# Row maxima over 1024 keys from two double banks, three rotating banks instead of four, and four smaller edits to an attention and expert kernel

## The reference

```python
x = x + attention(layernorm(x))          # q, k, v: 256x256; rope on the last 256 tokens; softmax(q k / 4) v; output projection
h = layernorm(x)
scores = softmax(h @ gate_w.T)           # 16 experts; each takes its 128 best tokens of each sequence
x = x + sum over experts of (gelu(t @ Wg.T) * (t @ Wu.T)) @ Wd.T * score     # t: the tokens taken
      + (gelu(h @ Ws_g.T) * (h @ Ws_u.T)) @ Ws_d.T                           # shared expert, all tokens
```

## Time and profile before

| | before |
|---|---|
| time, three runs | 2406.83 us median (2402.03 to 2407.79) |
| profiled execution | 2401.16 us, its span 2399.3 us |
| busy over the span | PE 2218.2 us (92%), DVE 1883.3 us (78%), ACT 1561.1 us (65%), POOL 895.3 us (37%) |
| granted TensorE clock, mean | 0.976 |
| attention up to its last step | to about 1475 us |
| shared expert, matmuls | 1514 us to about 1795 us |
| experts | to the end |

### The profile page before, as it was taken

One profiled execution on the slowest core, in us unless ns is written; L12 is line 12 of the kernel. 1 busy time (PEld: TensorE's weight loads), 2 busy tenths in 40 slices (PEclk: granted clock), 3 DMA queues, 4 the chain that ended last, 5 costly groups with the idle time before them and its releaser, 6 DMA issues. The chain is left out here.

```text
span 2399.3 us, 42479 instructions
## 1 busy us (share of the span) xinstructions
PE 2218.2 (92%) x15630; PEld 1288.6 (54%) x15630; DVE 1883.3 (78%) x3505; ACT 1561.1 (65%) x3040; POOL 895.3 (37%) x1287
## 2 busy tenths in 40 slices
PE   4899999999999999999999987899997999999996
PEld 3233333333333333333343323788886888888886
DVE  4999999999999999999999994566663554555553
ACT  2499888898888898898898886333332343434332
POOL 4051362451451451542542230000004666666664
PEclk8799999999999999999999999899998999999998
DMA  4002013012022121111112111323223455454543
GB/s 112 5 25 34 17 41 69 17 48 62 16 62 50 29 63 34 34 58 34 34 43 32 34 43 38 132 87 97 79 71 104 90 112 115 87 111 109 108 94 36
DMA packets 206756, 147.81 MB, mean 62 GB/s; under 512 B 109952, under 2 KB 193792, under 8 KB 206592
## 3 DMA queue, kind: packets, MB, share of 16 engines
q1 hardware_dynamic: 182016, 112.08, 17.3%
q0 software_dynamic: 24576, 33.57, 8.1%
HBM read 78.50 MB, written 41.94 MB: 50 GB/s over the span
## 5 line engine op out<-in xcount | busy, mean ns | idle before, releaser
L515 DVE TENSOR_REDUCE sb_MX<-ring 128x1 f32<-128x512 f32 x2048 | 1281.9, 680 | 67.7 <-PE ring L800 51.5
L646 ACT ACTIVATE sb_PR<-rot 128x512 f32<-128x512 f32 x2048 | 1119.5, 608 | 145.7 <-PE rot L811 130.2
L800 PE MATMUL ring<-sb_KT,sb_QT 32*128 32x512 bf16 x2048 | 526.6, 391 | 92.3 <-DVE sb_MX L515 76.9
L822 PE MATMUL pv<-sb_PR,sb_VA 128*32 128x512 f32 x4096 | 546.5, 606 | 2.6 <-ACT sb_OT L696 0.6
L800 PEld LDWEIGHTS ring<-sb_KT,sb_QT 32*128 32x128 bf16 x2048 | 129.9, 91 | 707.4 <-DVE sb_MX L515 649.0
L811 PE MATMUL rot<-sb_QT,sb_KT 32*128 32x512 bf16 x2048 | 405.1, 386 | 0.9
L1113 ACT ACTIVATE ex_GL<-ex_gu 128x512 f32<-128x512 f32 x128 | 76.5, 597 | 348.6 <-PE ex_gu L63 346.4
L1180 DVE TENSOR_TENSOR ex_HF<-ex_GL,ex_gu 128x512 f32<-128x512 f32 x128 | 87.4, 682 | 252.0 <-ACT ex_GL L1113 252.0
L1077 POOL DMA_INDIRECT out<-ex_YS,ex_rows_out x128 | 208.9, 1632 | 44.1 <-issue 43.7
L1034 POOL TENSOR_TENSOR ex_pool_scratch<-identity 128x1 f32<-128x1 f32 x96 | 35.1, 366 | 472.4 <-POOLq L877 325.8
L61 PE MATMUL ex_gu<-ex_XH,weights_high 128*128 128x512 f32 x512 | 201.1, 393 | 2.4 <-DVE ex_XL L1172 2.4
(11 more groups left out here) (158 smaller groups left out, 4042.8 us busy)
## 6 DMA issues: line engine op xcount, KB each, us to landing
sb_XA<-x SPq DMA_DIRECT2D x8, 1024.0 KB, 5.7
sb_XR<-x SPq DMA_DIRECT2D x8, 1024.0 KB, 5.7
out<-sb_XR SPq DMA_DIRECT2D x8, 1024.0 KB, 4.6
xn<-sb_XN SPq DMA_DIRECT2D x8, 1024.0 KB, 4.4
sh_XG<-xn SPq DMA_DIRECT2D x16, 512.0 KB, 5.9
sh_X<-out SPq DMA_DIRECT2D x16, 512.0 KB, 5.2
weights<-WgT SPq DMA_DIRECT2D x16, 512.0 KB, 4.0
weights<-WuT SPq DMA_DIRECT2D x16, 512.0 KB, 6.4
```

The source lines that it names most:

```text
L515: nc.vector.reduce_max(MX[:, unit % 2, half, j, qt % 4:qt % 4 + 1], ring[m % RING][:], AX.X).then_inc(ring_done, 1)
L646: out = nc.scalar.activation(PR[V % P_STEPS][:, j, :], R[:], ACT.Exp, scale=0.25)
L800: nc.tensor.matmul(ring[m % RING][:], QT[g][r, P * qt:P * qt + P], KT[g][r, 512 * half:512 * half + 512], start=True, stop=True, tile_posi ...
L822: out = nc.tensor.matmul(pv_bank[head(j), :], VA[b % 2][:, kt, 4 * g + j, :], PR[V % P_STEPS][:, j, :], start=(kt == 0), stop=(kt == TT - 1))
```

## The change

- **Maxima.** The three ring banks become two tensors of two banks each (`ring`, [P, 1024]). A maximum is one reduction over 1024 keys from two matmuls of the same head; there are 1024 of them, two for a step, instead of 2048 and four. `join_halves` goes. `split_maxima` waits for the reductions themselves, and VectorE waits for `parts_ready` where it starts a unit.
- **Rotating banks.** `ROT` goes from 4 to 3.
- **TensorE's order in a step.** Row-wise and turned matmuls alternate: keys 0 to 511 of a check, turned head 0, keys 512 to 1023 of the same check and the same head, turned head 1; then `weigh_values`; then the same with the second check and turned heads 2 and 3.
- **Roots.** In the loop GpSimd computes the inverse roots (a power and one correction, six small operations at S = 7 and S = 27). Before the loop and in the tail VectorE keeps its Newton steps.
- **Turned tokens.** The turned second norm `XT` is also stored to device memory (`xn2T`, 1 MB for each sequence), and the shared expert loads its chunks from there. Its TensorE transposes go. ScalarE waits for that store at the first aot item of each later sequence.
- **Logits.** Four items of two 128-token tiles at S = 47 to 50 instead of two of four at S = 47 and 48. VectorE's and ScalarE's gate steps move two steps later.

```diff
-    ROT = 4
-    RING = 3
+    ROT = 3
+    RING = 2
-    CHECKS = 32 * UNITS * B
+    CHECKS = 16 * UNITS * B
...
-              43: (1, "k", 4), 44: (1, "q", 5), 45: (1, "k", 5), 47: (-1, "lg", 0), 48: (-1, "lg", 1),
+              43: (1, "k", 4), 44: (1, "q", 5), 45: (1, "k", 5), 47: (-1, "lg", 0), 48: (-1, "lg", 1), 49: (-1, "lg", 2),
+              50: (-1, "lg", 3),
...
     def check(m):
 
-        unit, n = m // 32, m % 32
-        return unit, (2, 3, 0, 1)[n % 4], n // 4 % 2, 4 * (unit % 2) + n // 8
+        unit, n = m // 16, m % 16
+        return unit, (2, 0, 3, 1)[n % 4], 4 * (unit % 2) + n // 4
...
-        ring = [ctx.enter_context(nc.psum_tensor(f"ring{i}", [P, 512], F32)) for i in range(RING)]
+        ring = [ctx.enter_context(nc.psum_tensor(f"ring{i}", [P, T], F32)) for i in range(RING)]
...
+            def store_turned(b):
+                sp.wait_ge(rot_done, done(("x2t", b, KH - 1, 1)))
+                sp.dma_start(d["xn2T"][bass.ds(b * H, H), :].rearrange("(k p) t -> p k t", p=P), XT[:]).then_inc(xt2_out, 16)
...
                 turn_maxima(n + 7)
                 if b < B - 1:
                     turn_maxima(n + 8)
+                if b:
+                    store_turned(b - 1)
...
+            def inverse_root(n, count):
+
+                y = rstd[n]
+                pool.wait_ge(mv_ready[n], count)
+                own.inc(nc.gpsimd.tensor_scalar(spread[:], mv[n][:, :, 1], EPS, None, ALU.add))
+                own.wait(pool)
+                own.inc(nc.gpsimd.tensor_tensor(y[:], spread[:], minus_half[:], ALU.pow))
+                own.wait(pool)
...
+                unit, j, qt = check(m)
+                if m % 16 == 0 and unit >= 2:
+                    dve.wait_ge(parts_ready, unit - 1)
+                dve.wait_ge(ring_full, 2 * m + 2)
+                nc.vector.reduce_max(MX[:, unit % 2, j, qt % 4:qt % 4 + 1], ring[m % RING][:], AX.X
                                      ).then_inc(ring_done, 1)
-
-            def join_halves(unit):
...
-                if more and 7 <= S <= 12:
-                    newton(0, 2 * (S - 7))
-                if prev and 26 <= S <= 31:
-                    newton(1, 2 * (S - 26))
...
+                    if kind == "aot" and b and h == 0 and half == 0:
+                        act.wait_ge(xt2_out, 16 * b)
...
-                m = 4 * (V + LEAD)
-                if m < CHECKS:
-                    score_rows(m)
-                    score_rows(m + 1)
-                if V >= 0:
-                    for j in range(2):
-                        score_turned(V, j)
+                m = 2 * (V + LEAD)
+                for n in range(2):
+                    if m < CHECKS:
+                        score_rows(m, n)
+                    if V >= 0:
+                        score_turned(V, n)
                 if V >= LAG:
                     weigh_values(V - LAG)
-                if m < CHECKS:
-                    score_rows(m + 2)
-                    score_rows(m + 3)
-                if V >= 0:
-                    for j in range(2, 4):
-                        score_turned(V, j)
+                for n in range(2):
+                    if m < CHECKS:
+                        score_rows(m + 1, n)
+                    if V >= 0:
+                        score_turned(V, 2 + n)
...
-                    sp.dma_start(XG[k % 2][:], rows("xn2", n)).then_inc(x_in[k % 2], 16)
+                        sp.wait_ge(xl_ready, n - 1)
+                    sp.dma_start(XG[k % 2][:], d["xn2T"][bass.ds(r * D, D), N * k:N * k + N].rearrange("(k p) t -> p k t", p=P)
+                                 ).then_inc(x_in[k % 2], 16)
...
-                    if not (last and k == K - 1):
+                    if not shared and not (last and k == K - 1):
                         turn_tokens(r if k < K - 1 else r + 1, (k + 1) % K)
```

More of the change, by code:

```diff
@@ L121, in attention @@
             + [("proj", B - 1, i) for i in range(TT)] + [("x2t", B - 1, h, half) for half in range(2) for h in range(KH)]
-            + [("lg", B - 1, half) for half in range(2)])
+            + [("lg", B - 1, n) for n in range(4)])
     ORDER = HEAD + [item for V in range(-LEAD, LAST)
@@ L210, in attention @@
         rstd_ready = [sem(f"rstd_ready{n}") for n in range(2)]
+        mv_ready = [sem(f"mv_ready{n}") for n in range(2)]
         xn_ready = [sem(f"xn_ready{h}") for h in range(2)]
@@ L326, in _ @@
             own = Tally(pool_own)
+            own.inc(nc.gpsimd.memset(minus_half[:], -0.5))
             for n in range(2):
@@ L454, in _ @@
                     clear_maxima(b + 1)
+                if more and S == 7:
+                    inverse_root(0, b + 1)
+                if b and S == 27:
+                    inverse_root(1, b)
                 if more and 13 <= S <= 16:
@@ L476, in gather_stats, with merge_stats @@
                     own.inc(nc.vector.bn_stats(stats[:, i, :], src[:, i, :]))
-            def merge_stats(n, tiles):
+            def merge_stats(n, tiles, last=False):
                 own.wait(dve)
                 for i in tiles:
-                    own.inc(nc.vector.bn_aggr(mv[n][:, i, :], stats[:, i, :]))
+                    step = nc.vector.bn_aggr(mv[n][:, i, :], stats[:, i, :])
+                    if last and i == tiles[-1]:
+                        step.then_inc(mv_ready[n], 1)
+                    else:
+                        own.inc(step)
             def newton(n, k):
@@ L592, in _ @@
                 if more and S in (4, 5):
-                    merge_stats(0, range(4 * (S - 4), 4 * (S - 3)))
-                if more and 7 <= S <= 12:
-                    newton(0, 2 * (S - 7) + 1)
+                    merge_stats(0, range(4 * (S - 4), 4 * (S - 3)), S == 5)
                 if prev and 21 <= S <= 24:
@@ L686, in empty @@
                 elif kind == "lg":
-                    _, b, half = item
+                    _, b, n = item
                     if b:
                         act.wait_ge(shifted_ready, b)
-                    out = nc.scalar.copy(LG[:, 4 * half:4 * half + 4, :], R[:, 0:4 * E].rearrange("p (t e) -> p t e", e=E))
+                    out = nc.scalar.copy(LG[:, 2 * n:2 * n + 2, :], R[:, 0:2 * E].rearrange("p (t e) -> p t e", e=E))
                 out.then_inc(rot_done, 1)
@@ L777, in fill @@
                 elif kind == "lg":
-                    _, b, half = item
-                    pe.wait_ge(rot_done, done(("x2t", b, 1, half)))
-                    for m in range(4):
-                        i = 4 * half + m
+                    _, b, n = item
+                    pe.wait_ge(rot_done, done(("x2t", b, 1, n // 2)))
+                    for m in range(2):
+                        i = 2 * n + m
                         for h in range(KH):
@@ L789, in head, with score_rows @@
                 return slice(QUAD * j, QUAD * j + QUAD)
[L791 to L793 removed]
+            def score_rows(m, half):
+                unit, j, qt = check(m)
                 b, g = unit // UNITS, unit % UNITS // 2
[L795 removed]
+                if m % 32 == 0 and half == 0:
                     pe.wait_ge(qk_turned[g], 32 * (b + 1))
[L797 removed]
+                if m >= RING and half == 0:
                     pe.wait_ge(ring_done, m - RING + 1)
                 r = head(j)
[L800 removed]
+                nc.tensor.matmul(ring[m % RING][:, 512 * half:512 * half + 512], QT[g][r, P * qt:P * qt + P], KT[g][r, 512 * half:512 * half + 512],
                                  start=True, stop=True, tile_position=(r.start, 0)).then_inc(ring_full, 1)
@@ L882, in sem @@
             return ctx.enter_context(nc.semaphore(tag + name))
-        XG = [sb(f"XG{c}", [P, CT, D], F32) for c in range(2)]
+        XG = [sb(f"XG{c}", [P, KD, N] if shared else [P, CT, D], F32) for c in range(2)]
         XH = [sb(f"XH{c}", [P, KD, N], FR) for c in range(2)]
@@ L1107, in split_tokens @@
                 n = r * K + k
-                act.wait_ge(turned_full, n + 1)
-                nc.scalar.copy(XH[k % 2][:], turned[:, :, 0:N]).then_inc(xh_ready, 1)
+                if shared:
+                    act.wait_ge(x_in[k % 2], 16 * (r + 1))
+                    if not (isinstance(n, int) and n < 2):
+                        act.wait_ge(gu_full, KF * (n - 1))
+                    nc.scalar.copy(XH[k % 2][:], XG[k % 2][:]).then_inc(xh_ready, 1)
+                else:
+                    act.wait_ge(turned_full, n + 1)
+                    nc.scalar.copy(XH[k % 2][:], turned[:, :, 0:N]).then_inc(xh_ready, 1)
             def gelu(n, f):
@@ L1334, in down @@
                 out.then_inc(y_full, 1)
-            turn_tokens(0, 0)
+            if not shared:
+                turn_tokens(0, 0)
             if shared:
```

57 lines of the change are left out of this document (26 added, 31 removed).

## The result

The changed kernel takes 2497.59 us (median of four runs, 2495.69 to 2516.54). The kernel before, run beside it, takes 2405.57 us (2402.03 to 2407.79). The ratio is 1.0402, 95% interval 1.0349 to 1.0454: slower by 4%. The forecast was 2500.0. The profiled execution of after took 2495.69 us, its span is 2493.7 and its mean granted clock 0.971 (before: 0.976).

What follows compares the result with a forecast made beforehand. DVE, near 97% busy, looked like the bound; after the change the rot-bank loop and PE would set the steps. 2401.2 + 92.4 + 8 + 13 - 2 - 13 + 1 = 2500.6, forecast 2500 us, range 2430 to 2540.

Steps and rivals of the forecast that it cites:

- Three banks: Attention steps: the loop through three rot banks takes 2.45 us, or 2.94 through the fourth exponential, whatever DVE's relief.
- Two matmuls of one head: Attention steps on PE: the second matmul waits 0.21 us for its strip, twice a step; one projection goes to 2.97.
- Maxima: DVE in attention: a maximum goes from 0.62 to about 1.14 us, bounds 1.13 and 1.24, a step from 2.47 to 2.28.
- Sum for a middle sequence: Its 64 steps total 189.2 us, plus 2 for late waits: 191.2 against 175.8; six sequences +92.4.
- Sequence 0 and the last: First and last sequences of attention, with fewer items: +8 us in sequence 0 and +13 in the last.
- Roots: Power operation on GpSimd in the loop: taken as 0; +5 us a sequence if the power took 10 us.
- Turned store: New 1 MB store: 0, or 2 to 3 us a sequence if late; shared expert without transposes: -13 us.
- Tail: End of attention: the last store lies beside the logits and gates, +1 us.
- DVE sets the pace: Rival: DVE still bounds attention, so each sequence gives back about 16 us; 2268 us, chance 0.08.
- Banks late and the matmuls side by side: Rival: banks bind but matmuls of one head overlap; 187 us a sequence, 2482 us, chance 0.15.
- Matmuls queue and the banks don't bind: Rival: matmuls of one head queue, banks don't bind; 179 us a sequence with waits, 2408 us, chance 0.07.
- The store or GpSimd late: Rival: late waits cost 3 us more for each of 7 sequences; 2521 us, chance 0.10.

Runs made afterwards that it cites:

- the kernel with the shorter product: Changed kernel, but from the second unit on the products with the values cover only 256 of 512 queries: 2481.05 us, ratio 1.0312.
- the small edits alone: Changed kernel with banks, ring, order and 512-key maxima of before, leaving GpSimd roots, turned tokens and four logit items: 2368.85 us, ratio 0.9843.
- the added matmuls: Changed kernel with row-wise matmuls kept up in the last 12 steps, their results unread: 2500.36 us, ratio 1.0392.
- the kernel with half the maxima: Changed kernel, but VectorE's maximum reads only keys 0 to 511 of each check: 2502.51 us, ratio 1.0401.
- the other head: Changed kernel, but the second 512 keys of a row-wise check come from the neighbouring head: 2469.95 us, ratio 1.0267.
- the product last: Changed kernel with weigh_values moved behind the second half of a step's score matmuls, ahead of the items: 2597.76 us, ratio 1.0798.
- run 26: Not a run's number: the words belong to "a run 26 to 28 us below the profiled one", a distance in time.

## Why the prediction was right

- **The bound.** That the engine with 97% was not what mattered after the change holds: DVE at 85% waits for PE, and at half its work nothing moves.
- **Three banks.** The loop was put at 2.45 and measures 2.42, and 2.94 with one more exponential measures 2.91 (transposes). The handovers together were taken 0.03 too long. In the kernel with three banks alone, without DVE's relief, it is 2.94. Shown by that run, by the length of the product (0.43 less in each kind of step) and by the product's place.
- **Two matmuls of one head.** Put at 0.21 twice a step; it is 0.21 (0.53 against 0.32, behind the product), shown with banks and without. The projection step came out at 2.97 as forecast. The prediction did not weigh that the two costs cover each other: with maxima over 512 keys they cost 15.4 us a sequence together, and undoing the order alone gives back 0.6, undoing the bank alone 4.3.
- **Maxima.** A maximum is 1.22 us long. The bounds of 1.13 and 1.24 were for the distance between starts, and that is 1.15 where eight run in a row (in the kernel with the shorter product), as forecast. In after it decides no step, so its cost does not matter.
- **Sum for a middle sequence.** Steps alone 189.2 forecast, and by the table 14 x 2.42 + 2 x 2.58 + 22 x 2.97 + 5 x 3.40 + 9 x 2.91 + 3 x 3.06 + 3.40 + 7 x 3.54 + 3.23 = 188.2; with the single late wait of 0.7 us that is the measured 188.8 within rounding. I had added 2 for late waits and found 0.7: PE's wait for GpSimd's split at S = 24. So 13.0 a sequence, where I had 15.4, and 78.0 in six where I had 92.4. This is the term that was too large, by 1.0 in the steps and 1.3 in the waits. Longer steps give DVE more time, so most of its late waits are gone (S = 23 takes 3.14 before and with the small edits alone, and 2.91 in after). At S = 8 it is the moved roots that help: with the small edits alone the wait is gone too.
- **Sequence 0 and the last.** +8 became +10.5, and +13 became +16.2. In the last, 4.2 of that is clock, which the added matmuls took away again: 12.0 without it. How much it is differs between executions: in the kernel with half the maxima, which has the same matmuls in these steps, the last sequence took 184.2. What is above 8 in sequence 0 was not tried by itself.
- **Roots.** Taken at 0. The power costs 1.67 us on GpSimd, and what follows it is not late:

```profile
667.42 1.67 POOL L423 TENSOR_TENSOR sb_rstd<-sb_spread,sb_minus_half 128x8 f32<-128x8 f32 x1
```

- **Turned store.** Taken at 0, and it is: ScalarE waits for no transfer in attention. Shared expert -13, measured -12.4 (-13.4 alone). Experts -1.2, not forecast.
- **Tail.** +1 became +4.9. Most of it is the clock. The gate logits of the last sequence, in after:

```profile
1601.77 6.85 PE L807 MATMUL rot<-sb_gw,sb_XT 128*128 128x16 f32 x32
```

Before, the same 32 matmuls took 4.04 us. In the kernels with the other head and the product last they took 4.11 and 3.77, and the tail 43.8 and 42.5 us; with 6.85 it is 45.0 to 46.9. So 2.8 of the 4.9 are there, and some 2 stay open.

That the total is this close is luck. The sum, 2500.6, started from the profiled execution of before, and the one of after took 2495.7, 4.9 less. In this, errors cancel: -14.4 in the middle sequences and -1.2 in the experts against +2.5, +3.2 and +3.9 in sequence 0, the last and the tail, and +1.1 in the stretch to the first product and the shared expert. The median, 2497.59, lies 1.9 above that execution, and the base lay 4.4 below the median of before. The mechanism, and each kind of step to 0.05 us, is what the runs bear out.

**The rivals.** DVE sets the pace: out. (Its sum takes 15 us a sequence where its text says 16, which would give 2260 and not 2268.) Banks late and the matmuls side by side, 2482: this is the kernel with the other head, at 2470 and 185.5 us a sequence where the rival had 187 without late waits. In after the two do queue, so it is out as well. Matmuls queue and the banks don't bind, 2408: with four banks the order alone gives 186.9 a sequence at full clock and not 179. That kernel lacks the wide maxima, which 2.3 us in steps without an item would need; but its steps with two items took 3.36, and not the 3.2 I had put there. The store or GpSimd late: one wait of 0.7 us.

## What to carry to other kernels

Before taking work off the engine that is busiest, follow the loop through the buffers (who frees the bank that who needs for what) and price it without any wait: if it is as long as the present step, the relief is worth nothing, and a bank less can cost more than all of it. Two changes that each lengthen the same step cost about as much together as the longer one alone, so take back both, or little of the gain shows. Small matmuls that are issued in one group should each have rows of the array of their own. It does not help to put one on other rows between two on the same rows: here the turned matmul between the two starts at once with the first, and the second still starts 0.22 us later.

## What the runs showed of the hardware

**The first 160 us.** The same work got the full clock at different times after the start. The stretch from 100 to 160 us of the kernel with half the maxima, and then of after:

```profile
100.00:160.00 60.00, 60.00 (x280) 11.97 (x276) 21.32 (x34) 36.19 (x71) 17.57 (x30) 0.56 0.03 5
```
```profile
100.00:160.00 60.00, 57.39 (x399) 15.41 (x396) 53.92 (x55) 51.58 (x102) 22.54 (x35) 1.00 0.09 25
```

The work differs by half of each maximum. Yet the first is at 1.2 GHz from 50 to 153 us and the second from 50 to 98, and sequence 0 takes 196.8 and 174.6 us. The kernel with added matmuls in the last steps, whose work is that of after up to there, had 1.2 GHz from 48 to 160 us, with PE busy for all of the last 60, and 196.6 us for sequence 0. So 22 us lie between executions of the same work. Both of these kernels also have a run 26 to 28 us below the profiled one, so it falls differently from run to run. It probably explains the run of 2516.54 of after, of which there is no trace: its mean granted clock is 0.961, and 0.969 to 0.971 in the other three.

**The last steps and the shorter product.** At 1.96 us a step PE keeps 2.4 GHz in the last steps of before. With three banks the same steps are at least 2.39 long, and PE stands for a part of each: at full clock, in after it is busy for 6.37 of 8 us from 1550 to 1558, and in before for 10.45 of 11 from 1449 to 1460. Then the clock falls (after: 0.50 from 1559 to 1566 and from 1569 to 1579; three banks alone: from 1563 to 1604, where ten steps of about 3.69 cost 13 us). With matmuls in the gaps it stays full to the end of the steps and falls first at 1601. But it falls behind a busy PE too: in the shorter product PE was busy for 19.42 of 20 us just before 760, and in three sequences of the order alone the clock falls at the logits. What exactly brings it down, the runs don't settle.
